# Centring v without the fp32 product, and multiplying h by out_w on GpSimd between its row scatters

## The chip, the cores and the metric

The kernel runs on one core of one Trainium2 chip. A core has five engines that run side by side, each with its own queue of instructions in program order: TensorE (PE, matrix products, results into PSUM), VectorE (DVE), ScalarE (ACT), GpSimd (POOL, here fills, index lists and row scatters) and SyncE (SP, issues transfers). They wait for each other by semaphores only. The metric is the device time of one execution in microseconds (us).

## The reference, cut to what matters

32 sequences of 128 rows and 256 columns go through a cross-attention layer (an mLSTM cell, 8 heads of 32 columns) and then a layer of 8 experts, of which each row uses two.

```
xn = layernorm(x);  q = xn;  k = v = ctx                  # 8 heads of 32
ig, fg = gates([q, k, v]);  cs = cumsum(log_sigmoid(fg))
D = exp(cs_s - cs_t + ig_t - max_t(...)),  t <= s
C = (q k^T / sqrt(32)) * D
h = (C / (max(|sum C|, exp(-max)) + eps)) v
hn = (h - mean(h)) / sqrt(var(h) + 1e-5) * out_w          # mean, var over the 32 of a head
x1 = x + hn
out = x1 + experts(layernorm(x1))                         # 2 of 8 experts a row, gelu between
```

The mean of h over a head's 32 columns is taken away ahead of the product: the kernel centres v, and then the h that comes out is centred.

## The kernel before, in words

The 32 sequences go in 8 steps of four (S0 to S7; 0 to about 260 us), a software pipeline in which each engine has parts of up to four steps in its queue: `last`, `step`, `nxt` and `after`. The steps S0 to S2 and the beginnings of the next are written out by hand in `first_steps` of each engine; then `body(last, step, nxt, after)` runs five times, written out without a loop. Behind the steps, from about 245 us, the expert layer runs in tiles of up to 256 rows (`tile_turn` on PE, `turn` on DVE, `gelu` on ACT, `add_rows` on POOL). What sets the order on an engine is only the order of the calls in these functions.

What one step does, where the change touches it:

- `centre(step, r)` on PE, two calls a step, each for two sequences: v minus its head's mean goes into the PSUM bank `ps_h`. Before, a product of the fp32 unit matrix with the fp32 ctx (L1261) puts ctx itself there, and four fp16 products (L1264) of the two fp16 halves of ctx, turned, with `meanw` (-1/32 in the blocks of a head) take the mean off. `v_out` on ACT (L836) moves the bank to `vaug`.
- `scores`, `times_v` on PE, `c_of` on DVE (L1749: scores times decay, from PSUM and one SBUF tile, 128x1024), `h_out` on ACT give the unscaled h in `Hs` and its squares in `work`. PE must wait for `c_of(step, j)` before the next `scores` overwrite the bank, and before `times_v(step, j)`.
- `h_norm`, then `h_scaled` on DVE (the product of h with the scale of its head, L1780), `h_weighted` (times out_w, L1785, from two SBUF tiles), `x1_of` (plus x, L1792). `x1_stats` follows, and `write_x1` on SP.
- `choose` on DVE, eleven small instructions: which two experts a row takes; `records` ends with the row numbers `slot_i`.
- `scatter(step)` on POOL: an index list (L652), a wait for `records`, then eight indirect transfers (L662), for each of four sequences two (k = 0 and 1), that write rows into the table of the experts. The transfer of sequence j waits for that of j-1 with the same k. Beside these and the fills at the start POOL has nothing to do in the steps.
- `weights_low` on DVE (L1740: low halves of the expert weights, from two SBUF tiles) fills the rest of a step.

DVE's queue in one body, cut: `c_of(step, 2)`, ..., `c_of(step, 3)`, ..., `h_norm(step)`, `weights_low`, `h_scaled(step)`, `h_weighted(step)`, `choose(last)`, `gate_bias(after)`, `c_of(nxt, 0)`, `log_f(after)`, `x1_of(step)`, `c_of(nxt, 1)`, ..., `records(last)`.

PE's clock is granted by the chip and has two levels, 1.2 and 2.4 GHz; `stream` puts products that nobody reads into some waits of PE.

Of the kernel before, what the change touches and what calls it, by code (L numbers as in the profile page):

```python
# [5 lines left out]
ALU = mybir.AluOpType  # L6
# [7 lines left out]
P = 128  # L14
# [33 lines left out]
def build(nc, x, ctx_in, igate_w, igate_b, fgate_w, fgate_b, out_w, gate_w, w1, b1, w2, b2, out):  # L48
# [51 lines left out]
    with ExitStack() as ctx:  # L100
        def sb(name, shape, dt=F32):
            return ctx.enter_context(nc.sbuf_tensor(name, shape, dt))
# [27 lines left out]
        ident_h = sb("ident_bf16", [P, P], BF16)  # L130
        minus_h = sb("minus_ident_f16", [P, P], F16)
        never = sb("minus_big_above", [P, P], BF16)
        meanw = sb("minus_mean_of_head", [P, P], F16)
        pick = sb("pick_head", [3 * G, G], BF16)
        unpick = sb("minus_pick_head", [3 * G, G], BF16)
        runs = sb("a_and_running_max", [3 * G, 2, P])
# [198 lines left out]
        def number(step):  # L335
            return step[0] * 2 + step[1]
# [84 lines left out]
        with nc.Block() as block:  # L421
# [172 lines left out]
            def _(pool):  # L594
# [3 lines left out]
                pool.memset(tri_s[:, :], 1.0).then_inc(s_c0, 1)  # L598
                for zero in (ident_h, minus_h, never, pick, unpick):
                    pool.memset(zero[:, :], 0.0).then_inc(s_c0, 1)  # L600
                pool.memset(meanw[:, :], -1.0 / DH).then_inc(s_c0, 1)
                pool.wait_ge(s_c0, 9)
                pool.affine_select(out=ident[:, :], in_=ident[:, :], compare_op=ALU.not_equal, fill=1.0,
                                   base=0, pattern=[[-1, P]], channel_multiplier=1).then_inc(s_cp, 1)
# [11 lines left out]
                for n, (to, one) in enumerate(((pick, 1.0), (unpick, -1.0))):  # L616
                    for r in range(3):
                        if r:
# [1 line left out]
                        pool.affine_select(out=to[:, :], in_=to[:, :], compare_op=ALU.not_equal, fill=one,  # L620
                                           base=-G * r, pattern=[[-1, G]],
                                           channel_multiplier=1).then_inc(s_pick[n], 1)
                heads = meanw[:, :].rearrange("p (k e) -> p k e", k=HG)
                pool.affine_select(out=heads, in_=heads, compare_op=ALU.is_ge, fill=0.0, base=0,
                                   pattern=[[-DH, HG], [0, DH]], channel_multiplier=1).then_inc(s_mean, 1)
                pool.wait_ge(s_mean, 1)
                pool.affine_select(out=heads, in_=heads, compare_op=ALU.is_ge, fill=0.0, base=DH - 1,
                                   pattern=[[DH, HG], [0, DH]], channel_multiplier=-1).then_inc(s_cp, 1)
                for p in range(2):
                    pool.memset(vaug[:, p, :, :, DH:DH + 1], 1.0).then_inc(s_cp, 1)  # L630
                pool.iota(it_rev[:, :, :], [[0, SB], [-1, NE]], base=NE, channel_multiplier=0).then_inc(s_cp, 1)
# [9 lines left out]
                for p in range(2):  # L641
                    pool.memset(xfn[:, p, :, D:ROW], 0.0).then_inc(s_cp, 1)

                def scatter(step):
                    g = number(step)
                    if some(step, 2):
                        for done in s_sc[step[1]]:
                            pool.wait_ge(done, step[0] * SCATTERED)
                            pool.sem_inc(s_held, 1)
                    else:  # L650
                        pool.wait_ge(s_cp, 21)
                    pool.iota(xfn[:, step[1], :, F_TOK].bitcast(I32), [[S, SB]], base=g * SB * S,  # L652
                              channel_multiplier=1).then_inc(s_tok, 1)
                    pool.wait_ge(s_tok, g + 1)
                    pool.wait_ge(s_rec, g + 1)
                    pool.sem_inc(s_held, 1)
                    for j in range(SB):
                        for k in range(2):
                            if j:
                                pool.wait_ge(s_sc[step[1]][k], step[0] * SCATTERED + j * 16)  # L660
                                pool.sem_inc(s_held, 1)
                            pool.indirect_dma_start(  # L662
                                table, bass.IndirectOffsetOnAxis(ap=sloti[:, step[1], j, k:k + 1], axis=0),
                                xfn[:, step[1], j, :], None, bounds_check=TABLE - 1,
                                oob_is_err=False).then_inc(s_sc[step[1]][k], 16)

                def body(last, step, nxt, after):
                    if last is not None:
                        scatter(last)

                def first_steps():
                    scatter(S0)

                first_steps()
                run_steps(body, pool)
# [451 lines left out]
            def _(pe):  # L1127
# [121 lines left out]
                def centre(step, r):  # L1249

                    g = number(step)
                    pe.wait_ge(s_ql, g * SB + 2 * r + 2)
                    if r:
                        pe.wait_ge(s_vc, g * 2 + 1)
                    elif some(step, 2):
                        pe.wait_ge(s_hev, g * SB - SB)
                    elif some(step, 1):
                        pe.wait_ge(s_vc, g * 2)
                    for n in range(2):
                        j = 2 * r + n  # L1260
                        pe.matmul(ps_h[:, n * D:n * D + D], ident[:, :], ctxb[:, j, :], start=True, stop=False)  # L1261
                        for c in range(KC):
                            for a in range(2):
                                ins = pe.matmul(ps_h[:, n * D + c * P:n * D + c * P + P], qkT[:, step[1], j, a, KC + c, :],  # L1264
                                                meanw[:, :], start=False, stop=(c == KC - 1 and a == 1))
                    ins.then_inc(s_vm, 1)

                def times_v(step, j):
# [358 lines left out]
            def _(dve):  # L1627
# [32 lines left out]
                def gate_bias(step):  # L1660
                    g = number(step)
                    c_dg.begin(g)
                    f = gs[:, :, 1, :]
                    dve.wait_ge(s_gt, g + 1)
                    bias = gbias[:, :, :].rearrange("p a h -> p (a h)").unsqueeze(1).broadcast_to([P, SB, 2 * NH])
                    c_dg.link(dve, dve.scalar_tensor_tensor(
                        out=gs[:, :, :, :].rearrange("p j a h -> p j (a h)"),
                        in0=ps_gate.rearrange("p j a h -> p j (a h)"), scalar=1.0 / W_SCALE, in1=bias,
                        op0=ALU.mult, op1=ALU.add))
                    dve.scalar_tensor_tensor(out=nabs[:, :, :], in0=f, scalar=-1.0, in1=f, op0=ALU.mult,  # L1670
                                             op1=ALU.min).then_inc(s_na, 1)
# [111 lines left out]
                def h_weighted(step):  # L1783
                    dve.wait_ge(s_ho, number(step) + 1)
                    dve.tensor_tensor(work[:, :, :], work[:, :, :],  # L1785
                                      outw[:, :].unsqueeze(1).broadcast_to([P, SB, D]), ALU.mult).then_inc(s_hw, 1)

                def x1_of(step):
                    g = number(step)
                    dve.wait_ge(s_hw, g + 1)  # L1790
                    dve.wait_ge(s_xr, (g + 1) * 16)
                    dve.tensor_tensor(xres[:, :, :], xres[:, :, :], work[:, :, :], ALU.add).then_inc(s_x1, 1)  # L1792
# [123 lines left out]
                def body(last, step, nxt, after):  # L1916
                    if last is not None:
                        x1_norm(last)
                    if step is not None:
                        c_of(step, 2)  # L1920
                    if after is not None:
                        next_stats(after)
                    if nxt is not None:
                        weights_low(nxt, 0)
                    if after is not None:
                        next_norm(after)
                    if step is not None:
                        c_of(step, 3)
                    if nxt is not None:
                        next_a(nxt)  # L1930
                        weights_low(nxt, 1)
                        running_max(nxt)
                        split(nxt)
                        max_log_decay(nxt)
                    if step is not None:
                        h_norm(step)
                    if nxt is not None:
                        weights_low(nxt, 2)
                    if step is not None:
                        h_scaled(step)  # L1940
                        h_weighted(step)
                    if last is not None:
                        choose(last)
                    if after is not None:
                        gate_bias(after)
                    if nxt is not None:
                        c_of(nxt, 0)
                    if after is not None:
                        log_f(after)
                    if step is not None:  # L1950
                        x1_of(step)
                    if nxt is not None:
                        c_of(nxt, 1)
                        weights_low(nxt, 3)
                    if nxt is not None and after is None:
                        early_counts()
                        early_list()
                        c_of(nxt, 2)
                    if step is not None:
                        x1_stats(step)  # L1960
                    if last is not None:
                        records(last)

                def first_steps():
# [29 lines left out]
                    max_log_decay(S1)  # L1994
                    h_norm(S0)
                    h_scaled(S0)
                    h_weighted(S0)
                    c_of(S1, 0)
                    x1_of(S0)
                    gate_bias(S2)  # L2000
# [15 lines left out]
                    h_norm(S1)  # L2016
                    max_log_decay(S2)
                    h_scaled(S1)
                    h_weighted(S1)
                    x1_of(S1)  # L2020
                    c_of(S2, 0)
                    choose(S0)
                    gate_bias(S3)
                    x1_stats(S1)
                    c_of(S2, 1)
# [206 lines left out]
```

## Time and profile before

| | us |
|---|---|
| median of 3 executions (647.25 to 649.98) | 648.44 |
| the profiled execution | 651.1 |
| its span, first to last instruction | 649.1 |
| PE busy | 611.4 (94%) |
| DVE busy | 487.2 (75%) |
| ACT busy | 323.4 (50%) |
| POOL busy | 193.7 (30%) |
| mean granted PE clock, share of 2.4 GHz | 0.986 |

How to read the rows of the section further down. In a table of stretches a row is a stretch in us from the span's start, its length, then the busy time and number of instructions of PE, PE's weight loads, DVE, ACT and POOL, then the granted PE clock as a share of full speed, the DMA share and GB/s. In a table of waits a row is the waiting engine with its tile and line, behind the arrow what ended the wait, then us in total, times, and the longest. A row of the order in time is start and length in us, engine, line, operation, output and inputs, shapes, count, and in brackets the idle time before it and what ended it. An fp32 matrix product is recorded as two instructions, and a length of PE's rows includes its pipeline, so that distances between starts tell its pace.

### The profile page before, as it was taken

The numbers are of one execution on the slowest core, as the hardware profiler recorded it, in microseconds if no ns is written. First come the engines' busy times: TensorE is split into PE (matmuls) and PEld (weight loads), VectorE is DVE, ScalarE is ACT, GpSimd is POOL, SyncE is SP. The second block draws the span as 40 slices with busy tenths as digits, with TensorE's granted clock in tenths as the row PEclk, the third lists the DMA queues.
The fourth block names the chain that finished last, engine by engine and source line by source line (L and its number), as shares of the span: only waits on it lengthen the run. The fifth ranks groups of instructions, "written<-read, shape, count | busy, mean of one in ns | idle before, by whom it ended". The sixth has DMA issues, their size and how long they took to land. (4 is left out here: it accounts for less than half of the span.)

```text
span 649.1 us, 20273 instructions
## 1 busy us (share of the span) xinstructions
PE 611.4 (94%) x6736; PEld 526.6 (81%) x6737; DVE 487.2 (75%) x1330; ACT 323.4 (50%) x767; POOL 193.7 (30%) x185
## 2 busy tenths in 40 slices
PE   1799999999999899999999999999999999999995
PEld 1567777777777668998988988888989888989994
DVE  2546988999999898995888967666676757575684
ACT  2677888897988747544432323233232323232341
POOL 3000002242433424235345523232222323232333
PEclk9898998999999999999999999999999999999998
DMA  4443635475655626233464432323132323243510
GB/s 143 134 127 118 209 99 187 147 238 194 220 166 142 198 91 231 70 73 92 75 186 108 70 68 38 65 36 65 33 62 33 66 33 66 67 119 81 141 34 2
DMA packets 56044, 70.22 MB, mean 108 GB/s; under 512 B 5584, under 2 KB 50832, under 8 KB 55840
## 3 DMA queue, kind: packets, MB, share of 16 engines
q1 hardware_dynamic: 42560, 51.80, 26.3%
q0 software_dynamic: 13296, 17.32, 14.7%
q8 instruction: 49, 0.80, 0.5%
q14 instruction: 27, 0.22, 0.1%
q10 hardware_dynamic: 112, 0.08, 0.0%
HBM read 41.50 MB, written 24.92 MB: 102 GB/s over the span
## 5 line engine op out<-in xcount | busy, mean ns | idle before, releaser
L1059 ACT ACTIVATE decay_slots<-scores,b_turned 128x256 f32<-128x256 f32 (+1 forms) x312 | 124.4, 451 | 241.2 <-PE scores L1545 235.1
L1545 PE MATMUL scores<-x_slots,w_halves 128*128 128x256 f16 (+1 forms) x1760 | 193.7, 266 | 0.0
L1545 PEld LDWEIGHTS scores<-x_slots,w_halves 128*128 x1760 | 165.2, 98 | 17.3
L662 POOL DMA_INDIRECT expert_rows<-xf_rows,slot_i x64 | 71.9, 1124 | 211.8 <-issue 107.0
L1559 PE MATMUL pv<-w_halves,decay_slots 128*128 x864 | 97.6, 273 | 0.0
L684 POOL DMA_INDIRECT out_rows<-v_centred_and_one,row_ids x36 | 58.3, 1619 | 129.2 <-DVE v_centred_and_one L2146 95.7
L1559 PE MATMUL gate_bank<-w_halves,q_and_k_halves 128*128 x840 | 95.0, 273 | 0.0
L1559 PEld LDWEIGHTS pv<-w_halves,decay_slots 128*128 128x128 f16 x864 | 84.4, 98 | 9.7
L1559 PEld LDWEIGHTS gate_bank<-w_halves,q_and_k_halves 128*128 128x128 f16 x840 | 82.0, 98 | 9.5
L684 POOL DMA_INDIRECT out_rows<-work,row_ids x35 | 56.2, 1605 | 104.6 <-DVE work L2146 82.6
L1278 PEld LDWEIGHTS pv<-v_centred_and_one,decay_slots 128*128 128x128 f32 x512 | 63.7, 194 | 1.6
L1278 PE MATMUL pv<-v_centred_and_one,decay_slots 128*128 128x33 f32 x512 | 63.8, 260 | 0.0
L2133 DVE TENSOR_TENSOR decay_slots<-decay_slots 128x512 f16<-128x512 f32 (+1 forms) x80 | 51.2, 640 | 2.8
L2133 DVE TENSOR_TENSOR q_and_k_halves<-decay_slots,q_and_k_halves 128x512 f16<-128x512 f32 (+1 forms) x76 | 49.5, 651 | 2.6
L1740 DVE SCALAR_TENSOR_TENSOR w_halves<-weight_stage,w_halves 128x1024 f16<-128x1024 f32 x32 | 38.9, 1219 | 10.7 <-ACT w_halves L801 10.7
L789 ACT ACTIVATE decay_slots<-turn_bank 128x512 f32<-128x512 f32 x64 | 38.3, 598 | 8.6 <-PE turn_bank L1174 8.4
L1749 DVE SCALAR_TENSOR_TENSOR decay_slots<-scores,decay_slots 128x1024 f32<-128x1024 f32 x32 | 39.1, 1221 | 2.0 <-PE scores L1221 2.0
L2122 DVE CAST x_slots<-turn_bank 128x512 f16<-128x512 f32 (+1 forms) x39 | 25.1, 643 | 18.6 <-PE scores L1545 15.9
L1276 PE MATMUL pv<-minus_big_above,ident_bf 128*128 128x240 bf16 x128 | 34.8, 272 | 2.8 <-ACT work L810 1.7
L801 ACT ACTIVATE w_halves<-weight_stage 128x1024 f16<-128x1024 f32 x32 | 33.8, 1057 | 3.4 <-DMA weight_stage<-in_L_ffn_w 3.4
L2131 DVE CAST decay_slots<-decay_slots 128x512 f16<-128x512 f32 (+1 forms) x80 | 33.3, 416 | 2.0 <-ACT decay_slots L1059 2.0
L2131 DVE CAST q_and_k_halves<-decay_slots 128x512 f16<-128x512 f32 (+1 forms) x76 | 32.2, 423 | 0.1
(263 smaller groups left out, 864.5 us busy)
## 6 DMA issues: line engine op xcount, KB each, us to landing
weight_stage<-in_L_ffn_w SPq DMA_DIRECT2D x32, 512.0 KB, 4.0
x_slots<-in_x SPq DMA_DIRECT2D x16, 512.0 KB, 4.4
weight_stage<-expert_rows SPq DMA_DIRECT2D x30, 272.0 KB, 3.2
ctx_slots<-in_ctx SPq DMA_DIRECT2D x8, 512.0 KB, 6.0
out_rows<-x_slots SPq DMA_DIRECT2D x8, 512.0 KB
v_centred_and_one<-expert_rows SPq DMA_DIRECT2D x9, 272.0 KB, 3.0
expert_rows<-v_centred_and_one SPq DMA_DIRECT2D x9, 272.0 KB, 3.2
xf_rows<-w_halves SPq DMA_DIRECT2D x4, 512.0 KB, 4.1
```

The costliest lines, as they stand in the source:

```text
L662: pool.indirect_dma_start(table, bass.IndirectOffsetOnAxis(ap=sloti[:, step[1], j, k:k + 1], axis=0), xfn[:, step[1], j, :], None, bounds_ ...
L684: pool.indirect_dma_start(out_rows, bass.IndirectOffsetOnAxis(ap=ids[:, k, b:b + 1], axis=0), yo[k][:, b, :], None, bounds_check=T - 1, oo ...
L789: act.activation(E[:, j, HG * r:HG * r + HG, :].rearrange("p c s -> p (c s)"), ps_t[:, :], ACT.Exp).then_inc(s_ee, 1)
L1059: ins = act.activation(hf[:, f * R:f * R + tr.rows(0)], ps_s[:, q, n * R:n * R + tr.rows(0)], ACT.Gelu, bias=b1T[:, bass.ds(expert, 1), f] ...
L1276: pe.matmul(ps_h[:, P + P + 16:512], ident_h[:, :], never[:, 0:120].unsqueeze(1).broadcast_to([P, 2, 120]), start=True, stop=True)
L1278: ins = pe.matmul(ps_h[:, h * (DH + 1):(h + 1) * (DH + 1)], E[:, j, k * KC + u, :], vaug[:, step[1], j, h, :], start=True, stop=True)
L1545: ins = pe.matmul(o, w, xh[:, tr.slot(0) % 2, b, k, 0:tr.rows(0)], start=(n == 0), stop=(n == 3 * KC - 1))
L1559: ins = pe.matmul(ps_y[k % 2][:, c * D:(c + 1) * D], hh[k % 2][:, a, f, c * P:(c + 1) * P], w, start=(f == 0 and n == 0 and c == 0), stop= ...
L1740: dve.scalar_tensor_tensor(out=lo, in0=stage[:, half, :], scalar=W_SCALE, in1=hi, op0=ALU.mult, op1=ALU.subtract).then_inc(s_lo, 1)
L1749: dve.scalar_tensor_tensor(out=c, in0=ps_s[:, :, 0:KC * P], scalar=QK_SCALE, in1=c, op0=ALU.mult, op1=ALU.mult).then_inc(s_cm, 1)
L2131: dve.tensor_copy(hi, src).then_inc(s_hhi, 1)
L2133: dve.tensor_tensor(lo, src, hi, ALU.subtract).then_inc(s_hh, 1)
```

## The change

On PE the fp32 product of the unit matrix with ctx is left out. The matrix `meanw` becomes `centring`, one minus 1/32 on the diagonal and -1/32 beside it in a head's block, so that the same four fp16 products (eight a call) give the centred v itself; they read the fp16 halves of ctx in place of its fp32. A third selection on POOL at the start sets the diagonal.

The product of the scaled h with out_w moves from DVE to POOL for S0 to S6; for S7 DVE keeps it. On POOL it waits for `h_scaled` of its step, and `x1_of` on DVE waits for it. For S0 and S1 it stands ahead of the first scatter; for S2 to S6 between the seventh and the eighth transfer of the scatter of the step two before (`scatter(S0, S2)`, and `scatter(last, nxt)` in a body). In `first_steps` of DVE `x1_of(S1)` moves behind `c_of(S2, 0)` and `choose(S0)`.

```diff
@@ gpsimd
-                pool.memset(meanw[:, :], -1.0 / DH).then_inc(s_c0, 1)
+                pool.memset(centring[:, :], -1.0 / DH).then_inc(s_c0, 1)
...
+                pool.wait_ge(s_mean, 2)
+                pool.affine_select(out=centring[:, :], in_=centring[:, :], compare_op=ALU.not_equal,
+                                   fill=1.0 - 1.0 / DH, base=0, pattern=[[-1, P]],
+                                   channel_multiplier=1).then_inc(s_cp, 1)
...
-                def scatter(step):
+                def h_weighted(step):
+                    pool.wait_ge(s_ho, number(step) + 1)
+                    pool.sem_inc(s_held, 1)
+                    pool.tensor_tensor(work[:, :, :], work[:, :, :],
+                                       outw[:, :].unsqueeze(1).broadcast_to([P, SB, D]), ALU.mult).then_inc(s_hw, 1)
+
+                def scatter(step, beside=None):
...
                     for j in range(SB):
                         for k in range(2):
+                            if j == SB - 1 and k == 1 and beside is not None:
+                                h_weighted(beside)
...
-                        scatter(last)
+                        scatter(last, None if nxt == LAST else nxt)
...
-                    scatter(S0)
+                    h_weighted(S0)
+                    h_weighted(S1)
+                    scatter(S0, S2)
@@ tensor, centre
-                        pe.matmul(ps_h[:, n * D:n * D + D], ident[:, :], ctxb[:, j, :], start=True, stop=False)
                         for c in range(KC):
                             for a in range(2):
                                 ins = pe.matmul(ps_h[:, n * D + c * P:n * D + c * P + P], qkT[:, step[1], j, a, KC + c, :],
-                                                meanw[:, :], start=False, stop=(c == KC - 1 and a == 1))
+                                                centring[:, :], start=(c == 0 and a == 0),
+                                                stop=(c == KC - 1 and a == 1))
@@ vector, body and first_steps
                         h_scaled(step)
-                        h_weighted(step)
...
                     h_scaled(S0)
-                    h_weighted(S0)
                     c_of(S1, 0)
                     x1_of(S0)
...
                     h_scaled(S1)
-                    h_weighted(S1)
-                    x1_of(S1)
                     c_of(S2, 0)
                     choose(S0)
+                    x1_of(S1)
```

POOL's queue from the index list of S1 to that of S3, where `expert_rows` is the experts' table and `work` holds the scaled h; before:

```order
L652 IOTA xf_rows 128x4
L662 DMA expert_rows<-xf_rows,slot_i 35072x272 x8
L652 IOTA xf_rows 128x4
L662 DMA expert_rows<-xf_rows,slot_i 35072x272 x8
L652 IOTA xf_rows 128x4
```

and now, with the lines of the changed kernel:

```order
L662 IOTA xf_rows 128x4
L674 DMA expert_rows<-xf_rows,slot_i 35072x272 x7
L651 TENSOR_TENSOR work<-work,out_w_rows 128x1024
L674 DMA expert_rows<-xf_rows,slot_i 35072x272
L662 IOTA xf_rows 128x4
L674 DMA expert_rows<-xf_rows,slot_i 35072x272 x7
L651 TENSOR_TENSOR work<-work,out_w_rows 128x1024
L674 DMA expert_rows<-xf_rows,slot_i 35072x272
L662 IOTA xf_rows 128x4
```

Each scatter now has one product of `work` with the rows of out_w ahead of its eighth transfer.

DVE's queue in a body around `h_scaled` of a step (`h_slots` holds h, `route_bank` the router's scores, from which `choose` begins); before:

```order
L1633 SCALAR_TENSOR_TENSOR h_rstd<-h_newton,h_rstd 128x32
L1780 TENSOR_TENSOR work<-h_slots,h_rstd 128x1024
L1785 TENSOR_TENSOR work<-work,out_w_rows 128x1024
L1817 TENSOR_REDUCE top<-route_bank 128x4
L1818 TENSOR_TENSOR routing_work<-route_bank,top 128x32
L1819 SCALAR_TENSOR_TENSOR routing_work<-routing_work,rev_index 128x32
```

and now:

```order
L1647 SCALAR_TENSOR_TENSOR h_rstd<-h_newton,h_rstd 128x32
L1794 TENSOR_TENSOR work<-h_slots,h_rstd 128x1024
L1831 TENSOR_REDUCE top<-route_bank 128x4
L1832 TENSOR_TENSOR routing_work<-route_bank,top 128x32
L1833 SCALAR_TENSOR_TENSOR routing_work<-routing_work,rev_index 128x32
```

The product with out_w is gone between `h_scaled` and `choose`, and the rest keeps its order.

## Rows read from the trace of the kernel before

**Rows 1.** Table of stretches: two stretches of steady steps.
```profile
123.00:151.00 28.00, 26.49 (x381) 21.43 (x380) 26.35 (x79) 23.99 (x57) 9.99 (x10) 1.00 0.63 196
151.00:179.00 28.00, 26.48 (x382) 21.43 (x380) 26.34 (x76) 24.07 (x59) 10.00 (x11) 1.00 0.59 192
```

**Rows 2.** Table of waits, all engines, 123 to 206 us (three steps).
```profile
PE scores L1142 <- DVE decay_slots L1749: 3.1, 3, 1.0
...
PE scores L1221 <- DVE decay_slots L1749: 1.2, 3, 0.4
...
DVE square_sum L1759 <- ACT work L810: 0.6, 3, 0.2
```

**Rows 3.** Table of waits, DVE alone, 64 to 110 us.
```profile
DVE h_newton L1631 <- ACT h_rstd L721: 1.0, 1, 1.0
...
DVE decay_slots L1749 <- PE scores L1221: 0.2, 1, 0.2
```

**Rows 4.** Order in time, the first 40 us: ACT, PE and DVE.
```profile
13.39 1.06 ACT L801 ACTIVATE w_halves<-weight_stage 128x1024 f16<-128x1024 f32 x1 [3.40 <-DMA weight_stage<-in_L_ffn_w]
...
29.53 0.61 PE L1167 MATMUL turn_bank<-pick_head,three_parts 96*128 96x512 bf16 x1 [2.35 <-DVE three_parts L1717]
...
38.67 1.23 DVE L1749 SCALAR_TENSOR_TENSOR decay_slots<-scores,decay_slots 128x1024 f32<-128x1024 f32 x1 [1.83 <-PE scores L1221]
```

**Rows 5.** Order in time, PE: one call of `centre`.
```profile
144.89 0.59 PE L1261 MATMUL pv<-ctx_slots,ident 128*128 128x256 f32 x2
145.32 0.39 PE L1264 MATMUL pv<-minus_mean_of_head,q_and_k_halves 128*128 128x128 f16 x4
145.55 0.65 PE L1261 MATMUL pv<-ctx_slots,ident 128*128 128x256 f32 x2
146.03 0.39 PE L1264 MATMUL pv<-minus_mean_of_head,q_and_k_halves 128*128 128x128 f16 x4
```

**Rows 6.** Order in time, DVE in S4: `h_scaled`, `h_weighted`, first of `choose`, `c_of`.
```profile
173.16 1.23 DVE L1780 TENSOR_TENSOR work<-h_slots,h_rstd 128x1024 f32<-128x1024 f32 x1
174.41 1.23 DVE L1785 TENSOR_TENSOR work<-work,out_w_rows 128x1024 f32<-128x1024 f32 x1
175.56 0.18 DVE L1817 TENSOR_REDUCE top<-route_bank 128x4 f32<-128x32 f32 x1
...
178.27 1.22 DVE L1749 SCALAR_TENSOR_TENSOR decay_slots<-scores,decay_slots 128x1024 f32<-128x1024 f32 x1
```

**Rows 7.** Order in time, POOL: transfers 3, 4, 7, and two later sevenths.
```profile
164.39 0.97 POOL L662 DMA_INDIRECT expert_rows<-xf_rows,slot_i  x1 [2.31 <-DMA expert_rows<-xf_rows,slot_i]
165.79 1.60 POOL L662 DMA_INDIRECT expert_rows<-xf_rows,slot_i  x1 [0.43 <-issue]
...
173.89 1.33 POOL L662 DMA_INDIRECT expert_rows<-xf_rows,slot_i  x1 [0.48 <-issue]
...
201.93 1.95 POOL L662 DMA_INDIRECT expert_rows<-xf_rows,slot_i  x1 [1.12 <-DMA expert_rows<-xf_rows,slot_i]
...
228.97 0.97 POOL L662 DMA_INDIRECT expert_rows<-xf_rows,slot_i  x1 [0.53 <-issue]
```

**Rows 8.** Order in time, DVE: beside an idle POOL, and beside transfer 4.
```profile
57.05 0.29 DVE L1712 CAST three_parts<-a_and_running_max 96x256 bf16<-96x256 f32 x1
...
165.33 1.22 DVE L1740 SCALAR_TENSOR_TENSOR w_halves<-weight_stage,w_halves 128x1024 f16<-128x1024 f32 x1
...
167.11 0.40 DVE L1712 CAST three_parts<-a_and_running_max 96x256 bf16<-96x256 f32 x1
```

**Rows 9.** Order in time, POOL: two fills of different width.
```profile
0.87 0.20 POOL L596 MEMSET ident<- 128x128 f32 x1 [0.37 <-POOLq L2221]
...
261.01 0.34 POOL L695 MEMSET v_centred_and_one<- 128x272 f32 x1
```

**Rows 10.** Order in time, PE: a wait for a transfer.
```profile
109.05 0.66 PE L1142 MATMUL scores<-ident,x_slots 128*128 128x128 f32 x2 [1.21 <-DMA ctx_slots<-in_ctx]
```

**Rows 11.** Table of stretches: 4 us around that wait.
```profile
108.00:112.00 4.00, 2.95 (x15) 2.90 (x16) 3.65 (x9) 3.97 (x10) 0.97 (x1) 0.61 0.69 178
```

More of the change, by code:

```diff
@@ L132, in build @@
         never = sb("minus_big_above", [P, P], BF16)
-        meanw = sb("minus_mean_of_head", [P, P], F16)
+        centring = sb("one_minus_mean_of_head", [P, P], F16)
         pick = sb("pick_head", [3 * G, G], BF16)
@@ L622, in _ @@
                                            channel_multiplier=1).then_inc(s_pick[n], 1)
-                heads = meanw[:, :].rearrange("p (k e) -> p k e", k=HG)
+                heads = centring[:, :].rearrange("p (k e) -> p k e", k=HG)
                 pool.affine_select(out=heads, in_=heads, compare_op=ALU.is_ge, fill=0.0, base=0,
@@ L627, in _ @@
                 pool.affine_select(out=heads, in_=heads, compare_op=ALU.is_ge, fill=0.0, base=DH - 1,
-                                   pattern=[[DH, HG], [0, DH]], channel_multiplier=-1).then_inc(s_cp, 1)
+                                   pattern=[[DH, HG], [0, DH]], channel_multiplier=-1).then_inc(s_mean, 1)
+                pool.wait_ge(s_mean, 2)
+                pool.affine_select(out=centring[:, :], in_=centring[:, :], compare_op=ALU.not_equal,
+                                   fill=1.0 - 1.0 / DH, base=0, pattern=[[-1, P]],
+                                   channel_multiplier=1).then_inc(s_cp, 1)
                 for p in range(2):
```

## Prediction

> **What bounds the kernel now.** I read the table of stretches first, then who waits for whom, then the order in time of PE, DVE and POOL in one step. The names S0 to S7 are the eight groups of four sequences. In the steady steps (the two stretches of 28.0 us from 123 to 179) PE is busy 26.5 us and DVE 26.3 us, and ACT 24 [rows 1]: busy time alone names no bound. The waits do. In the three steady steps PE waits for DVE's product of scores and decay (`c_of`, L1749) at two places, 3.1 us and 1.2 us in all, while DVE waits only 0.6 us, for ACT [rows 2]. From 64 to 110 us it is much the same: DVE's longest wait is 1.0 us, for ACT, and for PE it waits 0.2 us [rows 3]. So DVE sets the pace from about 64 us to the end of the steps: what is taken from DVE shortens a step, and what is taken from PE lengthens its waits. Before that, the chains through PE count: DVE waited 1.83 us for scores at 38.67 [rows 4]. From about 260 us on the experts run, and nothing that the change touches is left there.
>
> **Part 1, the centring on PE.** One `centre` holds two pairs: an fp32 product of 0.43 or 0.48 us (144.89 to 145.32, 145.55 to 146.03) followed by four fp16 products in 0.23 us [rows 5]. The change drops the two fp32 products, and the fp16 ones stay eight. So each of 16 calls loses 0.43 + 0.48 = 0.91 us, 14.6 us of PE. Where is it worth anything? S0: behind its two calls PE waits for DVE, the last time 2.35 us up to 29.53 [rows 4]; covered, nothing. S1, first call: `scores` right behind it release the DVE product that waited 1.83 us [rows 4], so 0.9 us on the path. S1, second call: its reader, the evacuation on ACT, has other work ahead of it in ACT's queue; nothing. S2 to S7 lie in the stretch that DVE paces [rows 2, 3]; nothing. Sum: -0.9 us, with 14.6 us as the end that would hold only if PE were the bound, against [rows 2], and nothing as the other end. One more selection on POOL at the start is covered: ACT, on which the first tiles of x hang, waits 3.40 us for weights up to 13.39 [rows 4].
>
> **Part 2, the product with out_w leaves DVE.** In a steady step `h_scaled` starts at 173.16, the product L1785 at 174.41, and `choose` behind it at 175.56 [rows 6]: from 173.16 to 175.56 are 2.40 us, of which 1.14 (the pitch of such instructions back to back) would be left. The step is 1.26 us shorter. Seven of eight steps lose it: 7 x 1.26 = -8.8 us, all on DVE's path.
>
> **Part 3, what it costs on POOL.** No row shows a product of two tiles on POOL. The nearest: a fill of 128 columns takes 0.20 us and one of 272 takes 0.34 [rows 9], 0.97 ns a column. One pass over 1024 columns is then 1.1 us, two operands fetched one after another 2.1, two reads and a write one after another 3.1. I take 2.1, the middle one, since the product has two operands of that width and the fill none. By the Trainium skill (GPSIMD Engine Reference, section 3.1) an addition of two fp32 tiles of 2048 columns takes 4497 ns on GpSimd, from which I estimate 2.25 us for 1024, and the sum below would be 1.0 us higher.
>
> It matters who may read SBUF meanwhile. POOL's scatter that starts at 164.39 takes 0.97 us. The one at 165.79 takes 1.60 and so ends 0.84 us after DVE's weight product of 165.33, which reads two SBUF tiles [rows 7, 8]. The one at 173.89 takes 1.33 us and ends 0.83 us after `h_scaled`, another such [rows 6, 7]. So POOL's read waited for the end of DVE's two-input instruction, twice the same. The other way round, the cast at 167.11, begun while POOL's transfer ran, took 0.40 us against 0.29 at 57.05, when POOL was idle [rows 8]. The two engines exclude each other in both directions, for short reads. That a DVE instruction with two SBUF operands waits out a whole POOL product I read from this; no row shows it, and the other end is that they alternate and DVE loses nothing. The Trainium skill (SBUF — State Buffer, section "Who interferes with whom") says that such a DVE instruction and a GpSimd instruction that reads SBUF exclude each other for the whole instruction; by that rule the sum is the one below. The trace agrees as far as its short reads go.
>
> Where the product falls is set by the seventh scatter of the step two before, behind which it is queued; nobody waits for the eighth before the table is read. The product starts when the seventh ends, in S4 at 173.89 + 1.33 = 175.2 [rows 7], and would end at 177.3. DVE is then in `choose` and `gate_bias`, which before filled 175.56 to 178.27 [rows 6] and now begin 1.26 us sooner, from 174.3 to 177.0; six of the eleven small instructions of `choose` read two SBUF tiles. So DVE stands for about 2.0 us. S2 and S3 repeat this pattern: their seventh scatter, too, ends 0.83 us after `h_scaled`. In S5 the seventh starts at 201.93 and ends at 203.9 [rows 7], about 1.2 us later against DVE's order, with the end of `choose` and a two-input step of `gate_bias` left: 1.9 us. In S6 it ends at 229.9 [rows 7], as DVE enters `c_of`, which reads PSUM and one SBUF tile and which I count as not held, but the sum `x1_of` behind it, due about 1.1 us later, must wait until 232.1: 1.2 us. S0 has only one `c_of` (1.14 us) between `h_scaled` and `x1_of`: 1.2 us of waiting. S1 has `c_of` and `choose` in between and no scatters ahead: about 0.65 us. Sum: 1.2 + 0.65 + 3 x 2.0 + 1.9 + 1.2 = +10.9 us.
>
> **The sum.** -0.9 - 8.8 + 10.9 = +1.2 us. The profiled execution took 651.1 us (649.1 of span and 2.0 around it), 2.7 more than the median of 648.4. With 1.2 added it is 652.3, and the median 649.6. What is late next is PE: it reaches `scores` behind the second `centre` 1.8 us earlier and finds DVE about 0.8 us later, so it waits some 2.6 us there. A shorter one, 1.21 us for ctx up to 109.05 [rows 10], was followed by a granted clock at the lower level of 1.2 GHz, 0.61 of full speed on average from 108 to 112 [rows 11]: of 4 us PE gave 2.4 us' worth, and lost 1.6. I cost this at nothing, because DVE waits for no scores at all in the steady steps [rows 2], so that PE has both its old waits and the 1.8 us given back to be late in. Without that cover it is 1.6 us a step.
>
> **Rivals.** *The two engines don't hold each other, or only briefly.* Then of part 3 only the waits of `x1_of` stay: 1.2 (S0), 0.3 (S5), 1.2 (S6), and the sum is -0.9 - 8.8 + 2.7 = -7.0, 641.4 us. With exclusion but a product of 1.1 us, part 3 is 0.2 + 0 + 3 x 1.0 + 1.0 + 0.2 = 4.4, and the time 643.1. For it: rows 7 and 8 show only short reads, and POOL might give way between pieces. Against it: the cast, which waited. *The product is longer.* At 3.1 us, part 3 is 2.2 + 1.65 + 3 x 3.0 + 2.9 + 2.2 = 18.0, the sum +8.3, the time 656.7. The place is the same stretch of `choose` in S2 to S5 and the wait of `x1_of` in the rest; each further us costs about 7 us over the kernel, and from a product of 2.4 us on the kernel is slower by over 0.5%. *The work doesn't leave DVE's path at all*: POOL reaches the product late, since it stands behind transfers whose own waits differ (2.31 us ahead of 164.39, 0.48 ahead of 173.89 [rows 7]), so that one long wait moves it by 2 us. Then it meets `c_of`, holds nothing, and `x1_of` waits instead, 1 to 2 us a step: about 648.
>
> **How the numbers follow.** A difference of 0.5%, 3.2 us, is about what a measurement of this kernel can tell from no change. The forecast, exclusion with a product of 2.1 to 2.3 us, has 0.55: its own range is 647 to 653, of which 0.03 is faster, 0.39 within 0.5% and 0.13 slower (clock, or a product nearer to 2.4). No exclusion or a short product 0.24 (0.23 faster). A long product 0.16 (0.15 slower). A late product 0.05 (0.04 within). Together faster 0.27, same 0.45, slower 0.28. The range reaches from the first rival's 641.4 to just short of the second's 656.7: 641 to 655.5.
>
> **What would show it.** In the profile after: PE's fp32 rows of the centring gone, and some 0.44 us for eight products; L1785 gone from DVE in seven steps; on POOL a product of 2.1 us behind each seventh scatter, and beside it one small two-input instruction of `choose` that takes about 2 us instead of 0.19. If DVE's rows in `choose` keep their 0.19 us and the steps are 26 us long, exclusion is wrong and the first rival holds. If the product takes 3 us, the second does. If PE's waits for `c_of` don't grow, DVE was not the bound, and part 1 was worth more than I give it.

## The result

The changed kernel is slower: 675.25 us (median of 4 executions, 670.82 to 681.33) against 648.68 us, a ratio of 1.039 (95% interval 1.033 to 1.045). Executions more than 1.5% above the fastest of their kernel (here that of 681.33 us; of the kernel before three, one of them 1579.32 us long at a granted clock of 1.00, unexplained) count in the medians, but not in the ratios and in the means further down. The forecast was 649.6 us, and its range ended at 655.5.

| | before | after |
|---|---|---|
| median, us | 648.68 | 675.25 |
| profiled execution, span, us | 651.1, 649.1 | 670.82, 668.7 |
| PE busy, us | 611.4 | 615.5 |
| DVE busy, us | 487.2 | 488.2 |
| POOL busy, us | 193.7 | 209.3 |
| mean granted PE clock | 0.986 | 0.959 |

PE has some 14.6 us less to do (part 1 of the prediction) and is busy 4.1 us longer. The tables of stretches say why. After, with the last two rows for the steps and for the experts:

```profile
24.00:32.00 8.00, 4.44 (x19) 3.54 (x20) 4.71 (x19) 3.94 (x9) 0.00 (x0) 0.50 0.46 150
48.00:56.00 8.00, 7.51 (x78) 5.76 (x77) 1.32 (x2) 3.08 (x8) 0.00 (x0) 0.50 0.18 61
136.00:144.00 8.00, 7.08 (x60) 5.54 (x64) 7.58 (x26) 4.57 (x11) 2.24 (x4) 0.50 0.57 180
200.00:208.00 8.00, 7.31 (x58) 5.89 (x56) 7.18 (x19) 5.51 (x12) 3.91 (x4) 0.51 0.73 246
24.00:256.00 232.00, 202.76 (x2662) 157.75 (x2663) 182.46 (x500) 167.36 (x394) 63.66 (x53) 0.89 0.49 152
256.00:660.00 404.00, 403.09 (x3916) 362.03 (x3915) 296.28 (x789) 144.36 (x351) 136.49 (x96) 1.00 0.36 78
```

and of before, two of the same stretches and the steps:

```profile
24.00:32.00 8.00, 3.82 (x21) 2.70 (x20) 5.78 (x23) 3.90 (x10) 0.00 (x0) 0.68 0.47 135
48.00:56.00 8.00, 7.63 (x77) 6.30 (x78) 3.69 (x8) 4.09 (x9) 0.00 (x0) 0.79 0.28 84
24.00:240.00 216.00, 200.70 (x2749) 158.53 (x2748) 185.09 (x524) 169.33 (x398) 47.99 (x45) 0.97 0.53 164
```

The granted clock (third number from the right) is 0.89 of full speed over the steps instead of 0.97, and whole stretches of 8 us lie at 0.50, the level of 1.2 GHz. All of the loss is in the steps: `h_scaled` of S7 starts 19.0 us later than before, and from there to the end it is 396 us in before, 397 in after. The rows of `h_scaled`, before and after; behind the lengths of the eight in ns stand the first and the last start:

```profile
L1780 DVE TENSOR_TENSOR work<-h_slots,h_rstd x8: 1224/1225/1226, 64.0 to 252.9; 128x1024 f32<-128x1024 f32 x8
...
L1794 DVE TENSOR_TENSOR work<-h_slots,h_rstd x8: 1224/1225/1227, 67.0 to 271.9; 128x1024 f32<-128x1024 f32 x8
```

**Where the clock falls first.** Order in time of PE in S0, after:

```profile
21.65 0.61 PE L1277 MATMUL pv<-one_minus_mean_of_head,q_and_k_halves 128*128 128x128 f16 x8
24.83 0.64 PE L1209 MATMUL gate_bank<-log_sigmoid,tri 128*128 128x32 f32 x2 [2.57 <-DVE log_sigmoid L1692]
25.91 0.45 PE L1215 MATMUL gate_bank<-ident,i_minus_sum 128*96 128x128 f32 x1 [0.44 <-DVE i_minus_sum L1704]
28.65 0.61 PE L1181 MATMUL turn_bank<-pick_head,three_parts 96*128 96x512 bf16 x1 [2.29 <-DVE three_parts L1731]
```

and before, the first of the waits:

```profile
25.95 0.41 PE L1195 MATMUL gate_bank<-log_sigmoid,tri 128*128 128x32 f32 x2 [1.38 <-DVE log_sigmoid L1678]
```

The second `centre` of S0 (eight products, 0.61 us for all as recorded, no fp32) is over sooner, and PE waits 2.57 us for DVE where it waited 1.38 in before. The clock is then at 0.50 from 24 to 32 us, where before it was 0.68, and what PE does next, on which DVE waits in S0 and S1, takes longer.

**Where the product holds DVE.** POOL and DVE in S3, after:

```profile
158.09 2.36 POOL L651 TENSOR_TENSOR work<-work,out_w_rows 128x1024 f32<-128x1024 f32 x1 [1.14 <-DVE work L1794]
...
158.51 0.19 DVE L1832 TENSOR_TENSOR routing_work<-route_bank,top 128x32 f32<-128x32 f32 x1
158.74 1.76 DVE L1833 SCALAR_TENSOR_TENSOR routing_work<-routing_work,rev_index 128x32 f32<-128x32 f32 x1
160.53 0.19 DVE L1836 TENSOR_REDUCE xf_rows<-routing_work 128x4 f32<-128x32 f32 x1
```

The first instruction of `choose` with two SBUF operands takes 1.76 us and ends with POOL's product, at 160.45 to 160.50. Before, in S4, it took 0.19:

```profile
176.00 0.19 DVE L1819 SCALAR_TENSOR_TENSOR routing_work<-routing_work,rev_index 128x32 f32<-128x32 f32 x1
```

The one ahead of it, with one operand in PSUM, passes. In S4 the product, from 190.60 to 192.98, falls on an instruction of `log_f`, which takes 2.40 us instead of 0.18:

```profile
190.65 2.40 DVE L1692 SCALAR_TENSOR_TENSOR log_sigmoid<-gates,log_sigmoid 128x32 f32<-128x32 f32 x1
```

PE then waits three times, 0.7 to 0.95 us, the clock is 0.51 from 200 to 208 us, and the step takes 32.3 us instead of 27.4. In S2 it is worse, since the transfers ahead of the product were late (POOL, DVE, ACT and PE, one row each after the transfer):

```profile
131.12 0.97 POOL L674 DMA_INDIRECT expert_rows<-xf_rows,slot_i  x1 [0.66 <-issue]
132.10 2.36 POOL L651 TENSOR_TENSOR work<-work,out_w_rows 128x1024 f32<-128x1024 f32 x1
...
134.50 1.23 DVE L1806 TENSOR_TENSOR x_slots<-x_slots,work 128x1024 f32<-128x1024 f32 x1 [5.48 <-POOL work L651]
...
135.82 0.39 ACT L823 ACTIVATE h_slots<-pv 128x264 f32<-128x264 f32 x1 [5.33 <-DVE x_slots L1806]
...
136.92 0.83 PE L1235 MATMUL scores<-q_and_k_halves 32*128 32x128 f16 x24 [4.11 <-DVE decay_slots L1763]
```

`x1_of` waits 5.48 us for POOL, `c_of` stands behind it, PE waits 4.11 us for `c_of`, and the next 8 us run at a clock of 0.50.

### The profile page after: what moved, and what is told of

It is laid out like the page before. It is cut to its first block and busy times, and to the rows that moved or that the text cites. A ratio compares the mean times of both kernels' runs of the same rounds, so it can differ in the third digit from the quotient of the medians.

```text
span 668.7 us, 20154 instructions
## 1 busy us (share of the span) xinstructions
PE 615.5 (92%) x6672; PEld 527.1 (79%) x6673; DVE 488.2 (73%) x1323; ACT 323.1 (48%) x767; POOL 209.3 (31%) x193
## 3 DMA queue, kind: packets, MB, share of 16 engines
q1 hardware_dynamic: 42560, 51.80, 25.3%
## 5 line engine op out<-in xcount | busy, mean ns | idle before, releaser
L1559 PE MATMUL scores<-x_slots,w_halves 128*128 128x256 f16 (+1 forms) x1760 | 193.7, 266 | 0.0
L1292 PEld LDWEIGHTS pv<-v_centred_and_one,decay_slots 128*128 128x128 f32 x512 | 71.0, 213 | 1.8 <-issue 0.6
L1292 PE MATMUL pv<-v_centred_and_one,decay_slots 128*128 128x33 f32 x512 | 71.1, 275 | 0.0
L651 POOL TENSOR_TENSOR work<-work,out_w_rows 128x1024 f32<-128x1024 f32 x7 | 16.6, 2366 | 92.3 <-DVE work L1794 92.3
L1290 PE MATMUL pv<-minus_big_above,ident_bf 128*128 128x240 bf16 x128 | 36.7, 287 | 4.9 <-DVE decay_slots L1763 1.6
L2133 DVE CAST x_slots<-turn_bank 128x512 f16<-128x512 f32 (+1 forms) x39 | 25.1, 643 | 18.8 <-PE scores L1559 12.9
```

The costliest lines, as they stand in the source:

```text
L1290: pe.matmul(ps_h[:, P + P + 16:512], ident_h[:, :], never[:, 0:120].unsqueeze(1).broadcast_to([P, 2, 120]), start=True, stop=True)
L1292: ins = pe.matmul(ps_h[:, h * (DH + 1):(h + 1) * (DH + 1)], E[:, j, k * KC + u, :], vaug[:, step[1], j, h, :], start=True, stop=True)
L1559: ins = pe.matmul(o, w, xh[:, tr.slot(0) % 2, b, k, 0:tr.rows(0)], start=(n == 0), stop=(n == 3 * KC - 1))
```

## The experiments

For each kernel the table gives the median, the ratio to the kernel before on the same chip with its interval, and two means over its executions: the *lost clock* (span times one minus the mean granted clock) and the *rest* of the span. Lost clock counts also time in which PE only waits; it is an account, not a path. The kernel before has 7.8 and 639.9 us (49 executions, beside kernels 1 to 9).

| kernel | median | ratio (95%) | lost | rest |
|---|---|---|---|---|
| the whole change | 675.25 | 1.039 (1.033-1.045) | 33.1 | 638.4 |
| 1 centring alone | 664.71 | 1.018 (1.008-1.028) | 24.2 | 635.5 |
| 2 product alone | 664.99 | 1.026 (1.020-1.031) | 18.6 | 644.2 |
| 3 whole change, padded | 665.21 | 1.023 (1.015-1.031) | 18.8 | 644.0 |
| 4 centring, padded | 651.78 | 1.004 (1.001-1.007) | 8.3 | 640.6 |
| 5 centring, padded to S2 | 650.28 | 1.000 (0.996-1.003) | 7.3 | 640.4 |
| 6 unread product on POOL | 663.74 | 1.025 (1.017-1.032) | 19.9 | 642.8 |
| 7 unread fills on POOL | 648.61 | 0.999 (0.995-1.003) | 7.5 | 640.1 |
| 8 VectorE held | 660.72 | 1.018 (1.014-1.022) | 13.3 | 645.4 |
| 9 product early, padded | 668.65 | 1.028 (1.021-1.034) | 21.7 | 644.5 |

### The two halves apart (1 to 4)

Kernel 1 keeps the product on DVE:

> The changed centring alone; the product with out_w is back on VectorE at its old place. Theory C (clock): the change lost most of its time because a lightened TensorE waits more, falls to 1.2 GHz and makes VectorE wait for scores, as in the changed kernel, where 16 to 280 us hold 25.6 us of lost clock against 6.9 before. Then this kernel alone is 10 to 18 us slower than before, 659 to 667 us, with stretches of granted clock near 0.5 in the first 100 us. Theory W (waits for the product on GpSimd): the loss came from the late product and from the exclusion; then this kernel takes 646 to 650 us.

Kernel 2 keeps the fp32 product in the centring:

> The product on GpSimd alone; the fp32 product is back in the centring. Theory C: what is left are the holds that VectorE's rows show in the changed kernel, 1.1 (S0), 5.5 (S2), 1.6 (S3), 2.2 (S4), 1.6 (S5) and 2.9 us (S6), 14.9 in all, less the 8.8 us of the product itself: 6 us slower, 653 to 657 us. Theory W: nearly all of the loss, 668 to 676 us.

Kernels 3 and 4 put in the place of each fp32 product four bf16 products that nobody reads:

```diff
+                        for _ in range(4):
+                            pe.matmul(ps_h[:, n * D:n * D + D], ident_h[:, :],
+                                      never[:, :].unsqueeze(1).broadcast_to([P, 2, P]), start=True, stop=True)
                         for c in range(KC):
```

> The whole change, and in each pair of the centring four bf16 products of 256 columns that nobody reads, in the place of the fp32 product. Theory C: the clock holds as before and the time is that of the product on GpSimd alone, 653 to 657 us. Theory W: 672 to 678 us, as the whole change without them.

> The changed centring alone with the same four unread bf16 products in each pair. Theory C: as before the change, 647 to 651 us. Theory W: the same. If it is much slower than the changed centring alone, the unread products don't stand for the fp32 product, and the kernel with the whole change and the same products tells nothing.

Both halves lose, some 11 to 17 us each. The centring alone is 1.8% slower, and the unread products take that back but for 0.4%: it was the missing work of PE, not the new matrix. With them the whole change costs what the product alone costs. That is theory C for the centring. For the product neither theory held: 665 us, where C gave 653 to 657 and W 668 to 676.

### Where the centring needs its cover (5)

> The changed centring alone, with the unread TensorE products only in the six calls of S0 to S2. If TensorE's lost work matters only where the step is not yet paced by VectorE (the steps from S3 on were 27.4 us with the changed centring alone, as before), 649 to 654 us as with all of them. If the later calls matter too, 656 us or more.

650.28 us: the six calls of S0 to S2 are enough. In kernel 1 the steps S3 to S5 were 27.4 us, as before, and its `h_scaled` of S2 and of S7 start 12.9 us late alike. With the unread products PE's wait for DVE behind the second `centre` of S0, 2.57 us in kernel 1 as in the changed kernel, is 1.65 us. DVE's waits from 24 to 72 us, first with the centring alone, then padded to S2 (total, times, longest):

```profile
DVE max_log_d L1739 <- PE gate_bank L1219: 7.8, 2, 6.7
DVE log_f_sum L1699 <- PE gate_bank L1207: 7.4, 2, 6.7
DVE h_newton L1643 <- ACT h_rstd L733: 2.8, 1, 2.8
```
```profile
DVE max_log_d L1742 <- PE gate_bank L1219: 6.5, 1, 6.5
DVE log_f_sum L1702 <- PE gate_bank L1207: 3.4, 2, 2.9
...
DVE h_newton L1646 <- ACT h_rstd L733: 1.0, 1, 1.0
```

and PE's clock in 48 to 64 us, in the same order:

```profile
48.00:56.00 8.00, 7.51 (x77) 5.89 (x66) 1.32 (x2) 3.59 (x9) 0.00 (x0) 0.50 0.22 67
56.00:64.00 8.00, 8.00 (x44) 7.82 (x44) 5.74 (x11) 3.79 (x7) 0.00 (x0) 0.50 0.39 131
```
```profile
48.00:56.00 8.00, 7.71 (x93) 6.83 (x93) 5.07 (x11) 5.69 (x12) 0.00 (x0) 1.00 0.26 72
56.00:64.00 8.00, 7.50 (x86) 5.43 (x84) 6.63 (x16) 6.78 (x16) 0.00 (x0) 1.00 0.79 227
```

PE at half clock does 121 instead of 179 products (8 of these unread) in these 16 us, and DVE waits 3.8 us longer for the first gates of S1, 6.7 us against 2.9.

### What on POOL costs (6 and 7)

In the kernel before, DVE keeps its product, and POOL gets in S0 to S5 work for which no other engine waits, at the places of the change (kernel 6: a product of out_w with itself; kernel 7: two fills of 1024 columns in its place). The code of kernel 6, cut:

```diff
+                def unread(step):
+                    pool.wait_ge(s_ho, number(step) + 1)
...
+                    wide = outw[:, :].unsqueeze(1).broadcast_to([P, SB, D])
+                    pool.tensor_tensor(apart.rearrange("p (j d) -> p j d", j=SB), wide, wide, ALU.mult).then_inc(s_un, 1)
...
+                            if j == SB - 1 and k == 1 and beside is not None:
+                                unread(beside)
```

> The kernel before, with VectorE's product with out_w in its old place, and beside it a product of the same size on GpSimd whose result nobody reads, where the change has its own (S0 to S5; it multiplies out_w with itself). Nobody waits for it. Exclusion: in each of these steps one small two-operand instruction of VectorE, or x1_of, takes about 2 us longer, 8 to 12 us in all, and a fall of TensorE's clock may add 3 to 4: 657 to 664 us. No exclusion (the loss of the product on GpSimd is all waiting for a late result): 647 to 651 us.

> The same with two fills of 1024 columns on GpSimd in the place of each unread product: about as long, but they write only. If it is GpSimd's reads that hold VectorE, 647 to 651 us and VectorE's small instructions keep their 0.19 us. If any occupation of GpSimd holds it, as with the unread product, 657 to 664 us.

The product costs 14 us with no other engine waiting for it, the fills nothing. Order in time, POOL and DVE in S4 with the product:

```profile
178.14 2.15 POOL L652 TENSOR_TENSOR w_halves<-out_w_rows 128x1024 f32<-128x1024 f32 x1
...
178.90 1.44 DVE L1836 SCALAR_TENSOR_TENSOR routing_work<-routing_work,rev_index 128x32 f32<-128x32 f32 x1
```

and with the fills:

```profile
170.76 0.97 POOL L652 MEMSET w_halves<- 128x1024 f32 x1
171.88 0.95 POOL L652 MEMSET w_halves<- 128x1024 f32 x1 [0.15 <-POOL w_halves L652]
...
171.54 0.19 DVE L1836 SCALAR_TENSOR_TENSOR routing_work<-routing_work,rev_index 128x32 f32<-128x32 f32 x1
```

So it is POOL's reads that hold DVE, not the time for which it is busy. The Trainium skill (SBUF — State Buffer, section "Who interferes with whom") says that a DVE instruction with two SBUF inputs contends with a GpSimd instruction that reads SBUF, not with one that only writes it; both rows agree. But the holds that DVE shows here, 0.6 to 1.6 us a step, are some 6 us in all, and the kernel lost 14. In the table most of that is clock: the lost clock rose by 12.1 us, the rest by 2.9.

### A delay without POOL (8)

In S0 to S5 DVE does one more product that nobody reads, behind its product with out_w:

```diff
                     dve.tensor_tensor(work[:, :, :], work[:, :, :],
                                       outw[:, :].unsqueeze(1).broadcast_to([P, SB, D]), ALU.mult).then_inc(s_hw, 1)
...
+                    dve.tensor_tensor(apart.rearrange("p (j d) -> p j d", j=SB), wide, wide,
+                                      ALU.mult).then_inc(s_un, 1)
```

> The kernel before, and on VectorE behind its product with out_w one more of the same size (out_w with itself) whose result nobody reads, in S0 to S5. GpSimd does nothing new. Theory: any delay of VectorE in a step costs itself and then, since TensorE waits longer for VectorE, a fall of TensorE's clock on top. Delays: 6 x 1.14 = 6.9 us, so 655 to 657 us by the delays alone, and 660 to 665 us with the clock falls, the lost clock (span times one minus the mean granted clock) rising from 8 us to 13 or more. Rival: the clock falls come from GpSimd (transfers moved, or its reads); then 655 to 657 us and 8 us of lost clock.

6.9 us of delay cost 11.0 us, and the lost clock rose from 7.8 to 13.3 us. Four stretches of this kernel, each of which is at 1.00 in the kernel before:

```profile
72.00:80.00 8.00, 7.22 (x83) 5.72 (x87) 6.50 (x22) 6.09 (x15) 0.00 (x0) 0.79 0.87 308
96.00:104.00 8.00, 8.00 (x83) 6.25 (x84) 6.67 (x26) 4.01 (x14) 0.00 (x0) 0.62 0.01 2
136.00:144.00 8.00, 8.00 (x80) 6.89 (x81) 7.61 (x23) 6.57 (x16) 3.66 (x4) 0.79 0.69 212
168.00:176.00 8.00, 6.96 (x48) 6.21 (x47) 5.92 (x17) 6.14 (x14) 2.13 (x2) 0.79 0.63 179
```

PE waited 4.9 us for `c_of` from 123 to 210 us, six times up to 1.1 us, and the clock fell behind some of these waits. POOL had nothing new to do; whether the added product, with two SBUF operands, held POOL's transfers [rows 7] and delayed something by that was not tried apart. A delay of DVE thus cost more than itself, and the rise of the lost clock, 5.5 us, is half of the whole.

### The product ahead of the fifth transfer (9)

```diff
-                            if j == SB - 1 and k == 1 and beside is not None:
+                            if j == 2 and k == 0 and beside is not None:
```

> The whole change with the unread TensorE products in the centring, and the product on GpSimd ahead of the fifth transfer of the scatter, not of the eighth, so that it is never late. Lateness decides (x1_of waited 4.7 us in S2 and 2.0 in S6 with the same unread products, and clock falls followed): 652 to 657 us, no wait of x1_of for GpSimd over 1 us, and the steps are 28.3 us, 27.4 less 1.2 for the product and 2.1 more for the hold. Exclusion alone decides: 660 us or more, as without the move.

The product is never late now, S3 and S4 take 28.5 and 28.9 us, about the expected 28.3, and yet the kernel isn't faster: 668.65 us. Waits from 184 to 206 us:

```profile
ACT xf_rows L756 <- DMA expert_rows<-xf_rows,slot_i: 3.8, 1, 3.8
...
PE route_bank L1310 <- ACT xf_rows L756: 2.8, 1, 2.8
DVE newton L1648 <- ACT rstd L735: 2.5, 1, 2.5
```

POOL waits for `h_scaled` with four transfers behind it, the scatter ends later, and ACT, which is to write the next rows into that slot of `xf_rows`, waits for it; PE waits for ACT, and the clock is 0.61 from 192 to 200 us. The same wait of ACT comes again a step later, 3.5 us up to 227.8, and the clock is 0.50 from 232 to 248 us. The lateness was moved to another reader, so the kernel tells nothing of the price of lateness alone.

### Attempts at a faster kernel

All leave the product on DVE. Three used a wrong place: I took PE's wait for ctx at 108 us for that of S3, but it is that of S4, so that unread products or the product with v, moved in S1, only delayed S1 by 2 us.

> The changed centring alone with the unread TensorE products in each pair, and in the first steps the product with v of the last sequence of S1 ahead of the turning of S3, which waits for ctx. With the products alone, S0 and S1 were 2.9 us earlier than before, and that was lost again where TensorE waited 3.1 us for ctx at 108 us, its clock fell, and VectorE waited 4.9 us for the gates of S2. If that wait and its clock fall are what took the gain back, 644 to 648 us; if the gain is lost elsewhere, 650 to 653 us.

655.04 us, ratio 1.008 (1.004 to 1.011).

> The kernel before, with unread products of 512 columns in three waits of TensorE's first steps: six ahead of the sums of log f of S0, eight ahead of the first decay of S0, eight ahead of the turning of S3, which waits for ctx. If the falls behind these waits are most of what the kernel before still loses to the clock (8 us), 643 to 647 us. If the products cost more than the falls, 649 to 653 us.

655.28 us, 1.007 (1.003 to 1.010).

> The changed centring with unread products in the calls of S0 to S2, and the same products in the three waits. If the clock is all that held the changed centring back, 642 to 647 us, and no slower than the kernel before with those products; otherwise 649 to 654 us.

656.18 us, 1.011 (1.006 to 1.017). Three more had the right place, `times_v(S2, 3)` ahead of the turning of S4:

> The changed centring with unread products in the calls of S0 to S2, and in the first body TensorE's product with v of the last sequence of S2 ahead of the turning of S4, whose wait for ctx of 1.2 to 3.1 us ended at 108 us. If the clock fall behind that wait is a loss on the path, 645 to 649 us and a granted clock of 1.00 from 104 to 120 us; if it is covered or moves elsewhere, 649 to 652 us.

651.21 us, 1.000 (0.997 to 1.004).

> The same, and unread products of 512 columns in two waits of S0: six ahead of the sums of log f, eight ahead of the first decay. If keeping the clock from 24 to 40 us is worth what S0 gained with them elsewhere (its h_scaled came 1.3 to 2.5 us earlier), 643 to 647 us; if later waits take it back, 649 to 652 us.

651.12 us, 1.000 (0.997 to 1.003).

> The kernel before with both edits on TensorE and its old centring. If the gain of the other two is that of the clock alone, the same time as theirs within 1.5 us; if the changed centring adds something of its own, 2 us or more slower than the other with the same edits.

651.12 us, 1.001 (0.997 to 1.005). None beats the kernel before. The clock from 24 to 40 us was kept at 1.00 in the last two, `h_scaled` of S0 came 3 to 4 us earlier in their profiles (one execution each), and from `h_scaled` of S1 to that of S2 it took 30.7 and 30.5 us instead of 29.2, which gives back 1.3 to 1.5 us of that. Where the rest goes isn't shown; these two executions were themselves 1.6 to 2.1 us faster than their medians. The clock still fell from 104 to 120 us, behind a wait of 1.48 us for ACT that took the place of the one for ctx, in all three. What would keep it there stays open.

## Why the prediction was wrong, step by step

**What bounds the kernel.** Right from S3 on: with the centring alone S3 to S5 stay at 27.4 us. From 64 to 110 us it was true of the trace of before [rows 3], with nothing in reserve. After, in the same stretch, DVE waits for PE (total, times, longest):

```profile
DVE decay_slots L1763 <- PE scores L1235: 2.8, 4, 1.1
...
DVE log_f_sum L1701 <- PE gate_bank L1209: 1.8, 1, 1.8
```

**Part 1.** The work taken away was right, and so was "nothing" from S3 on. Wrong was "covered, nothing" for S0 and the step "I cost this at nothing, because DVE waits for no scores at all in the steady steps". That cover was read from S3 and later and used for the whole kernel. In S0 to S2 DVE waits for PE's gates, and the work that was removed lay ahead of waits of PE: removing it lengthened the first of them from 1.38 to 2.57 us, and the clock fell behind it. Instead of -0.9 the centring cost about 12 to 16 us; its rest fell by 4.4 us and its lost clock rose by 16.4. The hint stood in the prediction ([rows 10, 11]: a wait of 1.21 us, then 0.61).

**Part 2.** The 1.26 us leave DVE, but not all of it arrives: `choose`, now due sooner, waits for the router's scores from PE. In kernel 2, DVE in S3:

```profile
147.51 1.23 DVE L1791 TENSOR_TENSOR work<-h_slots,h_rstd 128x1024 f32<-128x1024 f32 x1
149.23 0.19 DVE L1828 TENSOR_REDUCE top<-route_bank 128x4 f32<-128x32 f32 x1 [0.49 <-PE route_bank L1315]
149.46 0.19 DVE L1829 TENSOR_TENSOR routing_work<-route_bank,top 128x32 f32<-128x32 f32 x1
149.68 2.36 DVE L1830 SCALAR_TENSOR_TENSOR routing_work<-routing_work,rev_index 128x32 f32<-128x32 f32 x1
```

From the start of `h_scaled` to `choose` are 1.72 us, before 2.40 [rows 6]: 0.68 saved, and a hold of 2.17. That is 27.4 - 0.68 + 2.17 = 28.89 us, and the step to the next `h_scaled` took 28.90. In the changed kernel that wait is 0.36 to 0.38 us in S2 to S5, 1.5 us together. What part 2 names nowhere is this: what is late next on DVE itself.

**Part 3.** Exclusion for the whole product, taken against the rival without it, was right. The product's price was 2.36 us instead of 2.1, and the rows of this case decide. From the Trainium skill's figure for 2048 columns, 4497 ns (GPSIMD Engine Reference, section 3.1), the estimate was 2.25. The cast from which the prediction read the other direction was weak evidence: in the kernel before it takes 0.40 us at 139.71, 167.11 and 194.51, but 0.29 at 111.04 and 219.85, beside a transfer each time. The holds:

| | S0 | S1 | S2 | S3 | S4 | S5 | S6 | sum |
|---|---|---|---|---|---|---|---|---|
| predicted, us | 1.2 | 0.65 | 2.0 | 2.0 | 2.0 | 1.9 | 1.2 | 10.9 |
| after, us | 1.1 | 0 | 5.5 | 1.6 | 2.2 | 1.6 | 2.9 | 14.9 |

`c_of`, with one operand in PSUM, isn't held, as assumed: in S1 it runs beside the product in 1.23 us. Of the 2.9 us in S6, 0.6 lie ahead of the product, beside the transfer before it. The late product, which had 0.05, came in S2, and I had priced it with the wrong sign: when the transfers slip by more than `choose` is long, nothing is excluded but `x1_of` waits 5.5 us, not 1 to 2. And "nobody waits for the eighth before the table is read" held in the changed kernel, where no wait of ACT for a transfer of the scatter shows, but not as such: kernel 9 shows the next user of `xf_rows` waiting for the scatter's end.

**The sum.** Parts 2 and 3 as measured give -8.8 + 1.5 + 14.9 = +7.6 us, 5.5 more than predicted. That leaves 19.0 of the 26.6 us for the term that I set to nothing, PE's clock ("I cost this at nothing"). The lost clock rose from 7.8 to 33.1 us, by 25.3; the centring alone raised it by 16.4, the product alone by 10.8. The 25.3 and the 7.6 us don't add up to the whole, since time in which PE waits at a low clock for a held DVE counts in both.

That a delay of DVE raises the lost clock without new work on POOL is shown by kernel 8, 5.5 us for a delay of 6.9. Kernel 6, with holds of some 6 us, raised it by 12.1: what makes the difference, the place of the holds or something else that POOL's reads do, stays open. That every single fall in the changed kernel has this cause is argued from the rows, not tried one by one.

## What to carry to other kernels

Before work is taken from TensorE, look at the wait behind that work in every phase, the first steps too: there it may be the work that keeps the clock, and unread products in its place show it in one run. A GpSimd product that reads SBUF held VectorE's instructions with two SBUF operands to its end (1.76 and 2.40 us instead of 0.19 and 0.18), so such an offload needs VectorE to be in work with an operand in PSUM, or idle, for just that time. On the engine that sets the pace a delay can cost more than its length, here 11.0 us for 6.9.

## What was not expected of the hardware

Span follows lost clock almost one to one: over the 49 executions of the kernel before that are counted above, which differ by up to 10 us, the span grows by 0.93 us for each us of lost clock (correlation 0.89). So much of the scatter between executions of this kernel goes with the clock, and a kernel's rest (639.9 us, standard deviation 1.0) is steadier than its time. Fills on GpSimd, 12 of 0.96 us beside VectorE's steps, cost nothing that can be measured (ratio 0.999, 0.995 to 1.003).
